# A graph layer on one core: the set-up's loads and VectorE operands rearranged, gathers allowed earlier, the last pairs reordered

## What is computed

```
h = relu(layernorm(x))                       # x: 12500 nodes x 32
e = concat([h[src], h[dst], edge_attr])      # 400000 edges x 96, dst is sorted
v = relu(e @ W1 + b1) @ W2 + b2              # 400000 x 32
out = x + maximum(segment_max(v, dst, 12500), h[:, -32:])
```

## Time and profile before

| | |
|---|---|
| median of 3 runs | 3227.99 us (3225.35 to 3228.82) |
| the profiled execution, its own time | 3226.88 us |
| its span | 3224.7 us |
| granted TensorE clock, mean | 0.971 |
| PE busy | 3004.2 us, 93% |
| DVE busy | 2190.4 us, 68% |
| ACT busy | 2111.5 us, 65% |
| POOL busy | 2415.8 us, 75% |

### The profile page before, as it was taken

The page is one execution under the profiler, slowest core; times in us unless marked ns, Lnnn a source line. Parts: engine busy times, 40 slices in busy tenths (PEclk is TensorE's granted clock), DMA queues, the critical chain, the costliest instruction groups (busy, mean ns, idle before and its releaser), DMA issues.

```text
span 3224.7 us, 56108 instructions
## 1 busy us (share of the span) xinstructions
PE 3004.2 (93%) x19600; PEld 2220.3 (69%) x19600; DVE 2190.4 (68%) x2400; ACT 2111.5 (65%) x2463; POOL 2415.8 (75%) x2547
## 2 busy tenths in 40 slices
PE   6999999999999999999999999999998998999910
PEld 4776677777777777777777777777776776777700
DVE  6221677777777777777777777777776776777643
ACT  2335677777777777777777777777776775777510
POOL 7777777777777777777777777777777777777756
PEclk9999999999999999999999999999999999999955
DMA  9930333333333333333333333333333323333221
GB/s 310 362 128 27 84 101 101 100 99 99 95 98 98 100 96 102 100 98 95 97 99 98 100 97 101 101 98 85 106 98 90 100 77 102 101 99 98 75 47 26
DMA packets 194363, 337.83 MB, mean 105 GB/s; under 512 B 74115, under 2 KB 118101, under 8 KB 193712
## 3 DMA queue, kind: packets, MB, share of 16 engines
q1 hardware_dynamic: 110520, 292.58, 26.5%
q0 software_dynamic: 81216, 41.73, 10.1%
q10 hardware_dynamic: 2482, 2.14, 0.2%
HBM read 227.85 MB, written 108.41 MB: 104 GB/s over the span
## 4 chain that ended last, share of the span: by engine, by line
PE 89%; POOL 3%; issue 3%; DMA 3%; DVE 2%; SPq 0%; ACT 0%; DVEq 0%; POOLq 0%; ACTq 0%
PE ps_rows L734 67%; PE ps_layers L713 4%; PE ps_layers L715 4%; PE ps_layers L748 3%; PE ps_layers L763 3%; PE ps_layers L772 3%; PE ps_layers L752 3%; POOL gathered_max L597 2%; PE ps_layers L758 2%; DMA picks<-picks_dram 1%; POOL src_in L524 1%; DVE onehot L969 1%; DMA gathered_max<-run_max,gather_ix 1%; DMA src_in<-h_dram,src_ix 0%; DMA dst_i<-in_dst_dram 0%
## 5 line engine op out<-in xcount | busy, mean ns | idle before, releaser
L524 POOL DMA_INDIRECT src_in<-h_dram,src_ix x2293 | 2166.4, 945 | 698.8 <-issue 635.4
L734 PE MATMUL ps_rows<-onehot,table 128*128 128x512 f32 x9800 | 2288.7, 393 | 22.1 <-DVE onehot L969 22.1
L734 PEld LDWEIGHTS ps_rows<-onehot,table 128*128 128x128 f32 x9800 | 1830.0, 188 | 496.6 <-issue 107.3
L665 ACT ACTIVATE onehot<-distance 128x1024 fp32r<-128x1024 bf16 x882 | 878.9, 1049 | 701.2 <-PE ps_rows L734 701.2
L660 ACT ACTIVATE distance<-picks,below_column 128x1024 bf16<-128x1024 int16 x882 | 954.7, 1136 | 36.8 <-DMA picks<-picks_dram 36.8
L969 DVE SCALAR_TENSOR_TENSOR onehot<-picks,column,ps_layers 128x1024 fp32r<-128x1024 int16 x392 | 493.0, 1278 | 365.3 <-PE ps_rows L734 345.9
L713 PE MATMUL ps_layers<-ea_t,rows_in 125*128 125x320 bf16 x980 | 269.0, 302 | 25.4 <-DVE rows_in L838 25.4
L1015 DVE STREAM_TRANSPOSE ps_layers<-rows_in 128x512 f32<-128x512 f32 x196 | 129.4, 705 | 221.2 <-ACT hid L651 191.5
L715 PE MATMUL ps_layers<-dst_t,rows_in 125*128 125x320 bf16 x980 | 268.9, 301 | 0.0
L651 ACT ACTIVATE hid<-ps_layers,b_col 128x512 f32<-128x512 f32 x392 | 234.1, 674 | 37.7 <-PE ps_layers L763 37.7
L1030 DVE TENSOR_TENSOR_SCAN max_t<-mask_in,max_t,ps_layers 128x512 f32<-128x512 bf16 x196 | 250.4, 1278 | 9.0 <-PE ps_layers L772 5.5
(11 more groups left out here) (106 smaller groups left out, 1049.3 us busy)
## 6 DMA issues: line engine op xcount, KB each, us to landing
picks<-picks_dram SPq DMA_DIRECT2D x98, 512.0 KB, 11.0
first_rows<-hid SPq DMA_DIRECT2D x100, 500.0 KB
rows_in<-in_edge_attr_dram SPq DMA_DIRECT2D x97, 512.0 KB
rows_in<-first_rows SPq DMA_DIRECT2D x97, 512.0 KB
run_max<-rows_in SPq DMA_DIRECT2D x96, 512.0 KB
src_in<-h_dram,src_ix POOLq DMA_INDIRECT x2293
mask_in<-mask_dram SPq DMA_DIRECT2D x97, 256.0 KB
h_dram<-h_sb ACTq DMA_DIRECT2D x1, 1568.0 KB, 6.6
```

What stands on the lines that cost most here:

```text
L524: pool.indirect_dma_start(out=src_in[:, slot, g, r, :], out_offset=None, in_=rows[:, :], in_offset=bass.IndirectOffsetOnAxis(ap=src_ix[:, ...
L665: nc.scalar.activation(onehot[:, RING_AT[c] + BY_DVE[c] + k, :, :].rearrange("p g w -> p (g w)"), distance[:, k, :], ACT.Relu, bias=1.0, s ...
L734: mm = nc.tensor.matmul(ps_rows[g][side][:, 0:WIDE], table[:, i * SIDES + side, part, :], onehot[:, RING_AT[c] + t, g, :], start=(i + part ...
```

## The change

`dst` is now the first load, on ScalarE's queue; `x` waits on SP until `dst` has landed; weights and picks move from ScalarE's queue to SP, behind the first three of the hundred clears; the mask is written after the twentieth. `dst_16` and its casts are gone. ScalarE copies the second operand of `rise`, of `mask` and of the table's remainder into PSUM, 512 columns at a time, over three banks, and VectorE takes it from there. ScalarE also makes `rise_hi`. The search begins tile by tile. `SLACK` is 6. The last pair's `dst_t` is filled before `turn_src(96)`, and `v` of the last two pairs goes to the look-up's banks. The core of the diff:

```diff
-SLACK = 3
+SLACK = 6
-SQUARE_AT, STD_AT, WRITE_AT = 3, 5, 7
+SQUARE_AT, STD_AT, WRITE_AT = 4, 6, 8
+CUT, CUT_BANKS = 512, 3
+TABLE_AT = [17, 18, 19, 22, 23, 24, 29]
@@ SP @@
-            sp.dma_start(dst_i[0:PIECE, SEARCH:SEARCH + BE], dst_rows[0:PIECE]).then_inc(dst_loaded, D)
-            sp.dma_start(dst_i[PIECE:BP, SEARCH:SEARCH + BE], dst_rows[PIECE:BP]).then_inc(dst_loaded, D)
             sp.dma_start(dst_i[1:1 + PIECE, 0:SEARCH], dst_before[0:PIECE]).then_inc(dst_loaded, D)
             sp.dma_start(dst_i[1 + PIECE:BP, 0:SEARCH], dst_before[PIECE:BP - 1]).then_inc(dst_loaded, D)
+            sp.wait_ge(dst_loaded, 4 * D)
             sp.dma_start(x_sb[0:PIECE], x_rows[0:PIECE]).then_inc(x_loaded, D)
...
             sp.wait_ge(zeros_made, 1)
-            clear(0, 20)
+            clear(0, 3)
+            for a in range(A):
+                sp.dma_start(pick_i[0:PAIRS - 2, :, a, :], bass.AP(src.tensor, STARTS[a] + GATHERED, [[2 * BLK, PAIRS - 2], [BLK, 2], [1, PICKED]])).then_inc(picks_read, D)
...
+            for a in range(A):
+                sp.dma_start(w_src[chunk(a), :], W1[0:F, :]).then_inc(weights_loaded, D)
...
+            clear(3, 20)
+            sp.wait_ge(mask_step, CUTS + 2)
+            sp.dma_start(mask_rows_out[0:PIECE], mask[0:PIECE, :]).then_inc(mask_written, D)
+            sp.dma_start(mask_rows_out[PIECE:BP], mask[PIECE:BP, :]).then_inc(mask_written, D)
             sp.wait_ge(h_written, D)
@@ ScalarE @@
+            act.dma_start(dst_i[0:PIECE, SEARCH:SEARCH + BE], dst_rows[0:PIECE]).then_inc(dst_loaded, D)
+            act.dma_start(dst_i[PIECE:BP, SEARCH:SEARCH + BE], dst_rows[PIECE:BP]).then_inc(dst_loaded, D)
...
+            for b in range(CUTS):
+                wait(act, rise_cut, b - (CUT_BANKS - 1))
+                at = cut(b)
+                nc.scalar.copy(ps_cut[b % CUT_BANKS][0:BP, 0:at.stop - at.start], dst_i[:, at]).then_inc(before_staged, 1)
+            for t in range(BT):
+                act.wait_ge(rise_cut, -(-(t + 1) * SEARCH // CUT))
+                nc.scalar.copy(rise_hi[:, t, 0:SEARCH], rise[:, t * SEARCH:(t + 1) * SEARCH]).then_inc(hi_made, 1)
@@ VectorE, set-up @@
-            V.tensor_copy(dst_16[:, :], dst_i).then_inc(rise_step, 1)
-            V.tensor_tensor(rise[:, :], dst_16[:, SEARCH:SEARCH + BE], dst_16[:, 0:BE], ALU.subtract).then_inc(rise_step, 1)
-            V.tensor_copy(rise_hi[:, :, 0:SEARCH], rises).then_inc(rise_step, 1)
-            V.tensor_tensor(rise_lo[:, :, :], rises, rise_hi[:, :, 0:SEARCH], ALU.subtract).then_inc(rise_step, 1)
+            for b in range(CUTS):
+                dve.wait_ge(before_staged, b + 1)
+                at = cut(b)
+                V.tensor_tensor(rise[:, at], dst_i[:, SEARCH + at.start:SEARCH + at.stop], ps_cut[b % CUT_BANKS][0:BP, 0:at.stop - at.start],
+                                ALU.subtract).then_inc(rise_cut, 1)
+            for t in range(BT):
+                dve.wait_ge(hi_made, t + 1)
+                V.tensor_tensor(rise_lo[:, t, :], rise[:, t * SEARCH:(t + 1) * SEARCH], rise_hi[:, t, 0:SEARCH], ALU.subtract).then_inc(lo_made, 1)
-            V.tensor_tensor(mask[:, :], dst_i[:, SEARCH:SEARCH + BE], dst_i[:, SEARCH - 1:SEARCH + BE - 1], ALU.is_equal).then_inc(mask_step, 1)
+            def same_dst(b):
+                dve.wait_ge(edge_staged, b + 1)
+                at = cut(b)
+                V.tensor_tensor(mask[:, at], dst_i[:, SEARCH + at.start:SEARCH + at.stop], ps_cut[b % CUT_BANKS][0:BP, 0:at.stop - at.start],
+                                ALU.is_equal).then_inc(mask_step, 1)
-                    V.tensor_tensor(table_f, table_f, table[:, :, part, :], ALU.subtract).then_inc(table_step, 1)
+                V.tensor_tensor(table_f[:, at, :], ps_cut[b % CUT_BANKS][:, 0:n * P].rearrange("p (t f) -> p t f", f=P), table[:, at, 0, :],
+                                ALU.subtract).then_inc(table_cut, 1)
@@ TensorE, last pairs @@
-                wait(pe, max_scanned, j * 2)
+                wait(pe, max_scanned, j * 2 - 2 if last else j * 2)
-                pe.wait_ge(dst_filled, j * 2 + 2)
+                pe.wait_ge(dst_filled, j * 2 + 2 if ahead else PAIRS * 2)
-                pair(PAIRS - 2 + slot, slot, ahead=False, last=slot == 1)
+                layer_one(PAIRS - 2 + slot, slot, False, slot == 1)
+                layer_two(PAIRS - 2 + slot, ps_rows[slot], True)
@@ VectorE, last pairs @@
+                if before_last:
+                    dve.wait_ge(onehot_made, PAIRS * DVE_ALL)
+                    dve.wait_ge(side_found, PAIRS)
+                    fill_dst(j + 2, slot, of_slot + 1, j + 1, last=True)
+            turn_edges(PAIRS - 1, 1, PAIRS // 2 - 1, last=True)
+            mask_rows(PAIRS - 1, 1)
+            turn_src(PAIRS - 1, 2 * AHEAD - 1, DOUBLE_TURNS - 1, last=True)
+            find_max(PAIRS - 2, 0, PAIRS // 2 - 1, True, ps_rows[0])
+            find_max(PAIRS - 1, 1, PAIRS // 2 - 1, True, ps_rows[1], LAST - BLK)
```

More of the change, by code:

```diff
@@ L621, in _, with stage_edge @@
-            for g, at in enumerate((GATHERED, BLK + LAST_GATHERED)):
-                act.dma_start(pick_i[PAIRS - 1:PAIRS, g, :, :], bass.AP(src.tensor, LANE - LAST + at, [[LANE, 1], [LANE, A], [1, PICKED]])).then_inc(picks_read, D)
+            def stage_edge(b):
+                wait(act, mask_step, b - (CUT_BANKS - 1))
+                at = cut(b)
+                nc.scalar.copy(ps_cut[b % CUT_BANKS][0:BP, 0:at.stop - at.start],
+                               dst_i[:, SEARCH - 1 + at.start:SEARCH - 1 + at.stop]).then_inc(edge_staged, 1)
@@ L623, in _ @@
+            for t in range(BT):
+                act.wait_ge(rise_cut, -(-(t + 1) * SEARCH // CUT))
+                nc.scalar.copy(rise_hi[:, t, 0:SEARCH], rise[:, t * SEARCH:(t + 1) * SEARCH]).then_inc(hi_made, 1)
+            for b in range(STAGED_FIRST):
+                stage_edge(b)
             act.wait_ge(node_ready, 2)
@@ L771, in layer_two, with pair @@
                     for a in range(A):
-                        mm = nc.tensor.matmul(ps_v[g][chunk(a), :], w_out[g * HID:(g + 1) * HID, :], hid[g * HID:(g + 1) * HID, a, :],
+                        mm = nc.tensor.matmul(v[g][chunk(a), :], w_out[g * HID:(g + 1) * HID, :], hid[g * HID:(g + 1) * HID, a, :],
                                               start=True, stop=True)
                 mm.then_inc(v_summed, 1)
[L776 to L779, removed]
+            def pair(j, slot):
+                layer_one(j, slot, True, False)
+                look_up(j + 2, slot, 0)
                 layer_two(j)
-                if ahead:
-                    for c in range(1, CHUNKS):
-                        look_up(j + 2, slot, c)
+                for c in range(1, CHUNKS):
+                    look_up(j + 2, slot, c)
             for j in range(2):
@@ L850, in _ @@
             V.tensor_tensor(centred, x_sb[:, :, :], ps_mean.unsqueeze(2).broadcast_to([P, NJ, F]), ALU.subtract).then_inc(ln_step, 1)
+            for b in range(STAGED_FIRST, CUTS):
+                same_dst(b)
+            dve.wait_ge(mask_step, CUTS)
+            V.tensor_scalar(mask[:, :], mask[:, :], 2 * BIG, -BIG, ALU.mult, ALU.add).then_inc(mask_step, 2)
             dve.wait_ge(ln_step, 4)
@@ L1010, in turn_edges, with fill_dst @@
                     V.transpose(of_half(ea_t[:, slot, :, :], h), ea_in[:, slot, h, :, :]).then_inc(ea_turned, 1)
+            def fill_dst(j, slot, turn, through, last=False):
                 dve.wait_ge(first_loaded[slot], turn * D + (A * D if last else D))
                 dve.wait_ge(mask_loaded[slot], turn * D + D)
-                wait(dve, hid_made, j * A)
+                wait(dve, hid_made, through * A)
+                wait(dve, dst_filled, j * 2)
                 for h in range(2):
@@ L1021, in turn_edges, with find_max @@
                                          ALU.min, ALU.max).then_inc(dst_filled, 1)
-            def find_max(j, slot, turn, again):
+            def find_max(j, slot, turn, again, v=ps_v, columns=BLK):
                 dve.wait_ge(v_summed, j + 1)
@@ L1028, in find_max @@
                 for g in range(2):
+                    n = columns if g else BLK
                     wait(dve, max_scanned, j * 2 + g)
-                    V.tensor_tensor_scan(max_t[:, g, :], mask_in[:, slot, g, :], ps_v[g][:, :], max_t[:, 1 - g, BLK - 1:BLK],
+                    V.tensor_tensor_scan(max_t[:, g, 0:n], mask_in[:, slot, g, 0:n], v[g][:, 0:n], max_t[:, 1 - g, BLK - 1:BLK],
                                          ALU.min, ALU.max).then_inc(max_scanned, 1)
```

167 lines of the change are left out of this document (97 added, 70 removed).

## The result

The kernel after takes 3221.91 us (median of 22 runs, 3218.38 to 3226.6) beside 3228.02 us (22 runs, 3225.2 to 3234.46) of the kernel before: ratio 0.9980, 95% interval 0.9974 to 0.9986. That is 6.1 us less, where 12.9 were forecast. Its profiled execution took 3222.25 us with a span of 3219.5, 4.6 us less than before.

The account below looks back on a forecast made before the run. GpSimd, full from 327.1 us, was taken as the bound late in the kernel. 3226.88 - 5.5 (GpSimd's set-up) - 7.4 (last pairs) = 3214.0 us profiled, median 3215.1; own range 3211 to 3219, 8 in 10 3209 to 3222.5.

Parts of the forecast that it names:

- the tail: Near the end, from GpSimd's last `src` gather to its first `run_max` gather; 7.4 us were to be saved there.
- First index load: Set-up: `dst` starting beside SP's index load delays GpSimd's first gather by 2.3 us, bounds 0 and some 5.
- `dst` sooner: Set-up: `dst` lands 3.5 us earlier, at 11 us, and TensorE starts look-ups about 6 us sooner, worth nothing at the end.
- VectorE's operands: GpSimd's early transfers: those held up under VectorE instructions with SBUF operands shorten, 8.7 us gained, bounds 0 and 13.9.
- The clears: Gate before GpSimd's first scatter: SP must clear everything and write start rows; last clear 4.5 us later, gate opens at 194.8.
- SLACK: GpSimd's lead over TensorE: 6 costs and gives nothing by itself, but keeps an advance of over 5 us from being lost.
- the burst that was named: GpSimd's fifth burst of the new turn, at 361.6 us, which with SLACK 3 needs pair 2's first tile, done at 362.3.
- The last pairs: End of the main loop: `layer_one(97)` no longer waits for `find_max(96)`, saving 7.4 us, bounds 4 and 8.5.
- the gate holds: Rival, 18 in 100: clears come 8 to 12 us later, GpSimd's saving goes into waiting for them; 3220.6 us.

Follow-up runs that it names:

- indices first: Kernel after, with `dst` on ScalarE's queue issued only once the index load has landed: 3217.86 us, ratio 0.9971.
- SLACK 3 and both edits: Kernel after, with `dst` held until the index load landed, picks and weights issued in turn with clears, and SLACK 3 instead of 6: 3215.84 us, ratio 0.9963.
- both edits: Kernel after, with `dst` held until the index load landed and picks and weights issued one by one between clears: 3216.49 us, ratio 0.9966.

## Why the prediction was right in sign and wrong in size

The forecast for the profiled execution was 3214.0 us; it took 3222.25, 8.2 more. GpSimd's last gather was forecast at 3063.5 and came at 3070.05, 6.5 us later; the tail was forecast at 24.19 - 7.4 = 16.8 and took 18.1, 1.3 more. These two are 7.8 of the 8.2. The median, 3221.9 us, lies outside the forecast's own range (3211 to 3219) and inside that of 8 in 10 (3209 to 3222.5), which had been widened for the rivals. The 0.78 given for faster by more than 6.5 us is also not what its terms add up to: 0.57 + 0.08 + two thirds of 0.26 = 0.82.

- **First index load: the step that failed.** I took 2.3 us for sharing the engines with `dst`, with 5 as the bound, on the ground that small rows share with few large ones. It cost 14.01 - 5.74 = 8.3 us in the profiled execution and 6.7 to 7.5 in the seven others with these loads. The queues took turns packet by packet, as the rows from 5 to 8 us show, so the small rows got 2% of the engines' time until the bulk of `dst` was through; and SP needed 3.38 us to issue the indices where it needed 1.95 before and with indices first. Holding `dst` back brought the first gather from 14.01 to 4.73 us and, over all profiles, cost `dst` some 1.3. The 5 us bound was half of a wait that itself began behind other loads; all of `dst`'s own time was the honest bound. The Trainium skill (DMA: Bandwidth & Descriptors, Queues, rings and completion order) says that each DMA engine goes round-robin between the queues with work for it, one whole packet of several descriptors at a time. By that rule a small load has no precedence over a large one on the other queue, and loses most where its own packets are short. The trace agrees: 66 packets beside 64, for 2.0% of the time beside 98.1.
- **`dst` sooner: failed too.** It was forecast at 9 to 13 us, sized at 11, and came at 14.12, where it was 14.48 before. Being first in the queue gained 0.4 us, up to 1.9 in the other profiles. What moved the search forward (first matmul at 20.43 instead of 25.37) was the work between, 6.3 us instead of 10.9, as estimated at 7. It was worth nothing at the end, as forecast.
- **VectorE's operands: right.** 7.1 us shorter, where 8.7 were taken; in the other profile of the same kernel it is 5.8 (12.92 to 202.00 us). The gathers of 4.16 and 3.89 us are gone, one of 2.78 us stays under `rise_lo` (L904), which keeps both inputs in SBUF, and three take 1.5 to 1.7. With two operands put back, gathers of 3.77 and 3.79 us came back under them. So the operand's place is the cause, not the instruction's length, and both are `tensor_tensor`: for indirect transfers the rows go against the inference in the Trainium skill (SBUF — State Buffer, Who interferes with whom) that the making of descriptors is free of such an instruction. Whether GpSimd stands with the reading of its indices or with the descriptors, no run here parts.
- **The clears: mis-sized, and without effect.** Start rows were issued at 198.54, 11.4 us later, where 4.5 were taken; in the other kernels with the same clears between 190.97 and 197.98, 3.8 to 10.8 us later. That spread of over 7 us between executions is not explained. The path to it was as worked out (fourth clear at 31.69, forecast 33.9 or 25.0), but the engines were as good as empty from 28 to 32 us (0.18 busy, 0.98 before), and that time was not made up. The gate was near GpSimd's own arrival at 201.5 in one profile and 7 us before it in another, and the first scatter came at 201.84 and 201.55. It was the binding one only once the indices came first: there GpSimd stood 3.9 us for it, and 1.5 us with SLACK 3 and both edits. With both edits the first scatter, 194.02 us, is within 1 us of the forecast's 194.8.
- **SLACK: right** at the usual clock: ratio 1.0002 alone, and with an advance of some 8 us SLACK 3 loses 3.6 us in one wait at the burst that was named, of which 2.75 remain from first scatter to last gather (2871.2 us for 2868.4). The kernel after has no such advance, so it has no use for it.
- **The last pairs: right in mechanism.** 7.4 us were forecast; alone, in the profiled execution, the tail fell from 24.19 to 16.90, 7.3 us. But that execution was the fastest of its eleven, and by medians the edit gave 4.7 us. The landing of the last gather was taken as 2.38 us from a row in the middle of the kernel. At the end it depends on the second load of `x`, which shares the engines with it: the last gather lands in 2.3 to 2.4 us when the load is out of the way, the one before it in 3.7 to 4.9 with the load some 6 us ahead, and in 7.0 to 8.2 with 2 to 3.
- **Rivals.** The outcome, 3221.9 us, is where "the gate holds" put it, and the size is that rival's: GpSimd's saving gone, the last pairs paying. But its mechanism was not this one: the saving went into waiting for the indices, before the first gather, not for the clears.

## What to carry to other kernels

A load that something waits for is not small beside a large one that another queue starts at the same moment: what counts is its number of packets and the length of the other's, and the small one can end with the large one. So chain them, and look what the large one loses. The same at the other end: a last gather's landing belongs to the critical path, and a bulk load issued a few microseconds ahead of it doubles or trebles it. When two gates nearly coincide, take each away alone and both together before saying which one costs.

## What was not expected of the hardware

The index load took 11.05 us of GpSimd's waiting with `dst` beside it (9.53 to 10.25 in other profiles at the usual clock) and 1.78 us with `dst` held back, while `dst` landed at 12.6 to 14.1 us in the first case and at 14.0 to 14.9 in the second. In the rows shown, packets of two queues passed one for one, at very unequal lengths. Indirect gathers landed in 2.3 to 8.2 us, those under a load of 1.56 MB 8.1 to 9.6 us after its issue. And one chip of the experiments' four ran the kernel before 35% slower, with pauses inside TensorE's work and a mean granted clock of 0.867, and there three kernels that are a little quicker elsewhere lost 9%.
